# Rotary swap of the first K and Q0 moved from TensorE products to VectorE half-by-half multiplies, with the splits, V rows and first projections reordered

## The reference

```python
Q = (x @ Wq.T + bq); K = (x @ Wk.T + bk); V = (x @ Wv.T + bv)   # per head: 32, 8 and 8 heads of 16
def rot_half(x):
    x1, x2 = jnp.split(x, 2, axis=-1)
    return jnp.concatenate([-x2, x1], axis=-1)
Q, K = q * cos + rot_half(q) * sin, k * cos + rot_half(k) * sin
w = softmax(Q @ K.T / 4)                       # four query heads per key/value head
x = layernorm(x + (w @ V) @ Wo.T + bo)
g = (x @ gate_w.T) * gate_s; u = (x @ up_w.T) * up_s
x = layernorm(x + ((silu(g) * u) @ down_w.T) * down_s)
```

## Time and profile before

| | |
|---|---|
| three runs | 1046.08, 1048.31, 1048.65 us |
| the profiled execution | 1047.48 us, its span 1045.6 us |
| PE busy | 1021.3 us (98%), 5858 matmul records |
| DVE busy | 795.0 us (76%) |
| ACT busy | 666.4 us (64%) |
| POOL busy | 278.5 us (27%) |
| mean granted TensorE clock | 0.995 |
| the chain that ended last | PE 92%, DVE 3%, DMA 2%, ACT 2% |

### The profile page before, as it was taken

The page is one execution under the profiler, slowest core; times in us unless marked ns, Lnnn a source line. Parts: engine busy times, 40 slices in busy tenths (PEclk is TensorE's granted clock), DMA queues, the critical chain, the costliest instruction groups (busy, mean ns, idle before and its releaser), DMA issues.

```text
span 1045.6 us, 15699 instructions
## 1 busy us (share of the span) xinstructions
PE 1021.3 (98%) x5858; PEld 536.3 (51%) x5858; DVE 795.0 (76%) x1139; ACT 666.4 (64%) x1346; POOL 278.5 (27%) x287
## 2 busy tenths in 40 slices
PE   8999999999999999999999998999999999999996
PEld 3643344433444433443444433333447888888885
DVE  4899978899778899779898898999703575563535
ACT  2359877789778889779666687888762431222221
POOL 2742021151345531246210155454000000000002
PEclk9999999999999999999999999999999999999999
DMA  5273517233125522444140447521327511312011
GB/s 203 81 209 109 118 36 215 54 98 90 53 65 127 99 81 40 86 100 104 35 79 12 117 149 155 142 81 34 113 81 198 137 41 41 81 45 37 1 40 43
DMA packets 64433, 94.88 MB, mean 91 GB/s; under 512 B 37536, under 2 KB 37920, under 8 KB 62272
## 3 DMA queue, kind: packets, MB, share of 16 engines
q1 hardware_dynamic: 63776, 93.10, 33.9%
q10 hardware_dynamic: 576, 0.72, 0.2%
HBM read 53.95 MB, written 27.00 MB: 77 GB/s over the span
## 4 chain that ended last, share of the span: by engine, by line
PE 92%; DVE 3%; DMA 2%; ACT 2%; issue 0%; SPq 0%; POOL 0%; POOLq 0%; DVEq 0%
PE PS L457 29%; PE PV L476 24%; PE PSA L546 15%; PE PSA L435 6%; PE PS L563 5%; PE PS L374 4%; PE PS L502 2%; PE PSA L502 2%; PE PV L563 2%; PE PSA L374 1%; PE PS L416 1%; ACT Bn L769 1%; DVE nmx L976 1%; DMA wr<-A 1%; DMA mscr<-mrow 1%; DVE nmx L972 1%
## 5 line engine op out<-in xcount | busy, mean ns | idle before, releaser
L769 ACT ACTIVATE Bn<-PS 128x512 f32<-128x512 f32 x1146 | 545.7, 558 | 102.7 <-PE PS L457 91.0
L457 PE MATMUL PS<-Qt,Kt 50*128 50x512 f32 x1146 | 392.0, 436 | 9.5 <-DMA Qt<-mscr 3.0
L435 PE MATMUL PSA<-Kt,Qt 48*128 48x512 f32 x1024 | 386.5, 460 | 1.2 <-DVE Kt L949 0.8
L972 DVE TENSOR_REDUCE nmx<-PSA 128x1 f32<-128x512 f32 x512 | 327.1, 678 | 33.7 <-PE PSA L435 33.7
L457 PEld LDWEIGHTS PS<-Qt,Kt 50*128 50x128 f32 x1146 | 187.3, 184 | 318.4 <-ACT Bn L769 296.8
L976 DVE TENSOR_REDUCE nmx<-PSA 128x1 f32<-128x1024 f32 x256 | 312.2, 1219 | 25.1 <-PE PSA L435 21.4
L476 PE MATMUL PV<-Bn 128*32 128x512 f32 x2048 | 274.2, 607 | 0.0
L435 PEld LDWEIGHTS PSA<-Kt,Qt 48*128 48x128 f32 x1024 | 175.4, 184 | 11.9 <-DVE nmx L972 3.3
L546 PE MATMUL PSA<-x1Th,wr 128*128 128x512 f32 x344 | 135.0, 393 | 1.1 <-DMA wr<-A 0.5
L546 PE MATMUL PSA<-x1Tl,wr 128*128 128x512 f32 x344 | 134.7, 392 | 0.0
L805 ACT ACTIVATE sg<-PSA,gs 128x512 f32<-128x512 f32 x43 | 29.6, 690 | 128.6 <-PE PSA L546 128.5
(11 more groups left out here) (167 smaller groups left out, 890.4 us busy)
## 6 DMA issues: line engine op xcount, KB each, us to landing
Qt<-pscr SPq DMA_DIRECT2D x90, 128.0 KB, 5.2
A<-in_wf SPq DMA_DIRECT2D x11, 768.0 KB, 7.1
wr<-A SPq DMA_DIRECT2D x33, 256.0 KB, 2.8
pscr<-A SPq DMA_DIRECT2D x16, 512.0 KB, 3.5
vscr<-Bn SPq DMA_DIRECT2D x32, 256.0 KB, 3.0
Kt<-pscr SPq DMA_DIRECT2D x90, 64.0 KB, 2.8
A<-A SPq DMA_DIRECT2D x16, 256.0 KB, 3.7
Bn<-vscr SPq DMA_DIRECT2D x8, 512.0 KB
```

What stands on the lines that cost most here:

```text
L435: op = e.matmul(PSA[:, 2 * s + h, :], Qt[n % 3][p:p + NC_, g % 2, 128 * qt:128 * qt + 128], Kt[n % 3][p:p + NC_, 512 * h:512 * h + 512], s ...
L457: e.matmul(PS2[:, i, cols], Kt[n % 3][rows, 128 * kt:128 * kt + 128], Qt[n % 3][rows, g % 2, 512 * qh + cols.start:512 * qh + cols.stop], ...
L769: e.activation(Pb[c % NP_][:, cols], PS2[:, score_bank[c, p], cols], ACT.Exp, scale=0.25).then_inc(*act_exp.next(piece(c, p)))
L972: e.tensor_reduce(col, slot_pair(s)[:, h, :], AX.X, ALU.max, negate=True).then_inc(*dve_max[s].next((k, 0) if h == 0 else k))
```

## The change

It takes the four permutation products away, with the matrix `swap` and its load. VectorE now exchanges the halves itself: `turn_pairs` multiplies partitions 0 to 63 of `raw` and of `sinT` and writes to partitions 64 to 127, and the other way round; the sign then is the other, so the add becomes a subtract. For (1,1) ACT makes two copies of 64 partitions from `raw`.

It moves `low_first(1, 0)` on DVE ahead of the placing of K. On ACT `round_x` of x comes piece by piece from the start of the program, `round_w(1)` stands ahead of the rounding of (1,0), and `evacuate(0, 1)` behind it. On POOL `low_x` starts with the first x, the wait for `dve_lo` is gone, and `low_w(1)` and `low_x(4, 5)` follow the third `cosines`. On PE a second product of ones with 256 columns stands behind the first one, two V rows stand ahead of the first group of maxima, the other six behind the first two groups, and the 16 projection steps are dealt out by twos and ones from the third group on. The picks of (1,1) use banks 1 and 3, and the first half of V bank 1.

```diff
-            def swap_pairs(i, h, ps):
-                w.wait_ge(*act_ev.at(("first", i, h)))
-                w.wait_ge(*landed["swap"].at())
-                e.matmul(ps, swap, cols_of(i, h)[0], start=True, stop=True).then_inc(*pe_swap.next((i, h)))
...
             e.matmul(PV[:, :], Vflat[:, 0:128], Vflat[:, 0:512], start=True, stop=True)
+            e.matmul(PV[:, 0:256], Vflat[:, 0:128], Vflat[:, 0:256], start=True, stop=True)
...
+            first_jobs = itertools.product(range(2), range(2), range(KT))
+            for k in range(8 + LEAD):
                 advance(4)
+                for t in range(3 * k + 2, 3 * k + 5) if k < 2 else ():
+                    value_rows(0, t, (1, 0)[t // 4])
                 if k == 4:
-                    for a, i in ((0, 2), (1, 3)):
+                    for a, i in ((0, 1), (1, 3)):
+                        clear(bank_free[i])
                         pick(1, 1, 2 + 2 * a, bank(i), pool_cs.at("lo"))
                         bank_free[i] = act_pick.at(("q", 1, a))
...
+                for _ in range((0, 0, 2, 2, 1, 2, 1, 2, 2, 1, 2, 1)[k]):
+                    j, h, part = next(first_jobs)
+                    project_half(j, h, ((2, 3), (0, 3))[j][h], (part,))
...
+            def swap_last():
+                raw, qrot, _, _ = cols_of(1, 1)
+                w.wait_ge(*act_ev.at(("first", 1, 1)))
+                for p in (0, 64):
+                    e.copy(qrot[64 - p:128 - p, :], raw[p:p + 64, :]).then_inc(*act_ev.next("swapped"))
...
-                w.wait_ge(*pe_swap.at((i, h)))
+                w.wait_ge(*act_ev.at(("first", i, h)))
                 w.wait_ge(*landed[f"sin{h}"].at())
-                e.tensor_tensor(qrot, ps, sin, ALU.mult).then_inc(*dve_rope.next(("swap", i, h)))
+                for p in (0, 64):
+                    e.tensor_tensor(qrot[64 - p:128 - p, :], raw[p:p + 64, :], sin[p:p + 64, :], ALU.mult).then_inc(
+                        *dve_rope.next(("swap", i, h)))
                 w.wait_ge(*dve_rope.at(("swap", i, h)))
                 w.wait_ge(*pool_cs.at((i, h)))
-                e.tensor_tensor(raw, rc, qrot, ALU.add).then_inc(*dve_rope.next((i, h)))
+                e.tensor_tensor(raw, rc, qrot, ALU.subtract).then_inc(*dve_rope.next((i, h)))
...
             e.memset(Vflat, 1.0).then_inc(*pool_one.next())
+            low_x(0, 1)
             cosines(0, 0, rcos[0])
+            low_x(2)
             cosines(1, 0, rcos[2])
+            low_x(3)
             cosines(0, 1, rcos[1])
-            w.wait_ge(*dve_lo.at((0, 1)))
             low_w(1)
-            low_x(0, 1)
+            low_x(4, 5)
```

More of the change, by code:

```diff
@@ L115, in post_ln_layer @@
         bo = A[:, 13312:13824]
-        swap = A[:, 13824:13952]
         sel_in = A[:, 13952:14720]
@@ L622, in tensor @@
             e.matmul(PV[:, :], Vflat[:, 0:128], Vflat[:, 0:512], start=True, stop=True)
+            e.matmul(PV[:, 0:256], Vflat[:, 0:128], Vflat[:, 0:256], start=True, stop=True)
             fill(0, 0, 0, 1, 2, 3)
[L624 to L629 removed]
+            fill(1, 0, 0, 1, 2, 3)
+            fill(0, 1, 0, 1, 2, 3)
             pick(0, 0, 0, PSA[:, 0, :], dve_lo.at((0, 0)))
[L631 to L632 removed]
+            fill(1, 1, 0, 1)
             for a in range(2):
                 pick(1, 0, 2 + 2 * a, bank(2 * a), dve_lo.at((1, 0)))
[L635 removed]
+            fill(1, 1, 2)
             pick(0, 1, 0, PSA[:, 1, :], dve_lo.at((0, 1)))
[L637 removed]
+            fill(1, 1, 3)
+            bank_free[0], bank_free[2] = act_pick.at(("q", 0, 0)), dve_pick.at(("q", 0, 1))
             first_rows = [[act_pick.at(("k", 1)), dve_pick.at(("k", 1)), act_pick.at(("q", 0, 0)), dve_pick.at(("q", 0, 1))],
                           [act_pick.at(("q", 1, 0)), act_pick.at(("q", 1, 1))]]
+            for t in range(2):
+                value_rows(0, t, 1)
             w.wait_ge(*act_pick.at(("k", 1)))
@@ L876, in scalar @@
             load(bqk[:, :], bqk_d, "bqk")
-            load(swap, sw_d, "swap")
             load(sel_in.rearrange("p (m c) -> p m c", m=6), sel_d, "sel")
+            round_x(0, 1)
             evacuate(0, 0)
@@ L881, in scalar @@
             e.copy(sel[:, :, :], sel_in.rearrange("p (m c) -> p m c", m=6)).then_inc(*act_pick.next("sel"))
+            round_x(2)
             round_first(0, 0, dve_rope.at((0, 0)))
             evacuate(1, 0)
+            round_x(3)
+            round_w(1)
+            round_first(1, 0, dve_rope.at((1, 0)))
             evacuate(0, 1)
             place(Kt[0][0:NC_, 0:512], PSA[0:NC_, 0, :], pe_pick.at((0, 0, 0)), ("k", 0))
-            round_first(1, 0, dve_rope.at((1, 0)))
+            round_x(4, 5)
             round_first(0, 1, dve_rope.at((0, 1)))
             place(Qt[0][:, 0, 0:512], bank(0), pe_pick.at((1, 0, 2)), ("q", 0, 0))
+            place(Kt[0][0:NC_, 512:1024], PSA[0:NC_, 1, :], pe_pick.at((0, 1, 0)), ("k", 1))
             evacuate(1, 1)
-            place(Kt[0][0:NC_, 512:1024], PSA[0:NC_, 1, :], pe_pick.at((0, 1, 0)), ("k", 1))
-            round_w(1)
-            round_x(0, 1)
-            w.wait_ge(*pe_swap.at((1, 1)))
-            e.copy(cols_of(1, 1)[1], PV[:, :]).then_inc(*act_ev.next("swapped"))
+            swap_last()
+            round_x(6, 7)
+            round_w(2)
             round_first(1, 1, pool_cs.at("rope"))
-            round_x(2, 3, 4, 5, 6, 7)
-            round_w(2)
             round_w(3)
-            for a, i in ((0, 2), (1, 3)):
+            for a, i in ((0, 1), (1, 3)):
                 place(Qt[0][:, a, 512:1024], bank(i), pe_pick.at((1, 1, 2 + 2 * a)), ("q", 1, a))
@@ L1235, in vector @@
                 maximum(next(steps))
-                if k in (2, 4):
-                    add_values(0, k // 4, k // 4)
+                if k in (1, 3):
+                    add_values(0, k // 2, (1, 0)[k // 2])
             for u in range(SPLIT):
@@ L1439, in gpsimd @@
                 *pool_cs.next("lo"))
-            low_x(2, 3, 4, 5, 6, 7)
+            low_x(6, 7)
             low_w(2)
@@ L1812 @@
         "ident": np.eye(128, dtype=np.float32),
-        "swap": np.roll(np.eye(128, dtype=np.float32), 64, 0),
         "sel": select_rows(),
```

47 lines of the change are left out of this document (8 added, 39 removed).

## The result

The changed kernel takes 1054.63 us (median of four runs, 1052.23 to 1054.98), the kernel before on the same chip 1047.91: ratio 1.0068, 95% interval [1.0055, 1.0081]. The profiled execution took 1054.41 us, its span 1052.6 us, 7.0 us more than the span before.

A forecast was written before the change was run, and what follows sets the result against it. PE is full from the main loop on, so its start decides. +4.2 (first maxima) +2.4 (clock) -2.0 (sweep) +1.0 (ACT's wait) = +5.6 on 1047.5, 1053.1, put at 1053.5 for the median; range 1043.3 to 1056.8 us.

The forecast's parts named there:

- Rival 1: DVE's meetings with POOL in the opening cost little: turns of 3.6 us, 1043 to 1044.7 us, faster; chance 0.25.
- Rival 2: DVE gets both multiplies in before POOL: turn 4.8 us, first maxima near 29, 1047.5 to 1051 us; chance 0.17.
- rival 3: Larger loss: POOL's instructions shut DVE out, or half clock lasts into sweep: +8 to +10, 1056 to 1058 us; chance 0.08.
- The multiplies: DVE in the opening: two of 0.69 us each per turn; without POOL a turn takes 3.6 us against 4.7.
- POOL between the turns: DVE's turns in the opening: DVE and POOL wait for each other, so turns take 5.8 us, the third 7.2.
- The series of turns on ACT: Opening: ACT evacuates (1,0) and (0,1) only behind the rounding of the piece before; called new, given no separate size.
- The second product of ones: PE at the program's start: filled idle time brings the clock's rise forward, 1.0 us; first fill ends at 10.6.
- First maxima: End of the opening's first part: 32.3 us against 28.1, so +4.2, with the clock's fall counted separately.
- the clock: PE's idle times in the opening bring half clock on picks, fills and V rows: +2.4 us, bounds 0 and 3.
- The sweep: From first maxima to main loop: 32.7 us against 34.7, so -2.0.
- What is late next: Start of the main loop: ACT waits 1.1 us for Q1's rotation with the exponentials queued behind, +1.0.

The follow-up runs named there:

- e1: The change with POOL's later splits (low_x(2) on, low_w(1)) put back behind the wait for DVE's remainder of (0,1); 1049.76 us, ratio 1.0021.
- e3: The change with POOL's later splits back behind the wait for DVE and evacuate(0, 1) on ACT ahead of the rounding of (1,0) again; 1047.65 us, ratio 1.0002.
- e7: The kernel before with only the three exchanges of (0,0), (1,0), (0,1) made by DVE multiplies instead of permutation products; 1047.93 us, ratio 1.001.
- e8: The kernel before with only the second product of ones (256 columns) added behind the first; 1044.5 us, ratio 0.9986.
- e4: The change with unread products of ones in PE's two long waits, ahead of the picks of (1,0) and (0,1); 1052.01 us, ratio 1.0046.
- e2: The change with evacuate(0, 1) on ACT again ahead of the rounding of (1,0), and round_w(1) behind it; 1054.78 us, ratio 1.0075.
- e6: e3 with the sweep dealt as in the kernel before; 1046.08 us, ratio 0.9996.
- e9: The kernel before with the second product of ones, low_x(0, 1) early on POOL, early rounding on ACT and a new dealing of the sweep; 1043.24 us, ratio 0.9964.
- e11: e3 with two unread products of 128 columns behind each group of maxima from the sixth on; 1046.56 us, ratio 1.0002.

## Why the prediction was right, point by point

The forecast was 1053.5 us, slower by 0.5%, through DVE and POOL standing in each other's way; measured were 1054.63. The direction and the mechanism hold. The kernels e1 and e3 show it by taking POOL's splits away: with all multiplies kept, DVE's last remainder ends at 24.35 and 24.58 us instead of 29.09, and the first maxima come at 27.71 and 27.95 instead of 33.85. What remains untested is the other half of the guard's worth: the kernel before with its permutation products and an unguarded POOL was not run. Rival 1 (the meetings cost little) is out by the rows of 1.65 and 3.42 us. Rival 2, both multiplies first, did not occur either: DVE's pair took 2.36 us even in the first turn. Of rival 3 its second half did come in small, half clock in the sweep, though in the projections and not in the V rows. That the total came out within 1.2 us is partly luck, since several terms below miss by about 1 us and more, in opposite directions. By its own steps:

- **The multiplies.** 0.69 us for 64 partitions was right: a pair that POOL leaves alone takes 1.40 (e7). The gain of 1.1 us per turn was not: with the cosines alone against it a turn is 4.5 us (e1, from DVE's start at 10.64 to 15.11), against 4.7 before.
- **POOL between the turns.** Forecast 5.8, 5.8 and 7.2 us from the evacuation's end to the remainder's; measured 5.45 (11.30 to 16.75), 5.7 (16.61 to 22.29) and 6.9 (22.16 to 29.09). I had every instruction wait for the next end of the other engine; a few were clear, such as the subtract of the second turn. The price per meeting had been read from two rows of which the second, at 1036.14, is a TENSOR_SCALAR and no TENSOR_TENSOR; the rows of the change now show it for the instruction in question: the subtract of the first turn, begun at 13.73, ends at 15.38, 0.55 us behind the end of POOL's at 14.83, as the remainder of the earlier trace rows did behind 22.43. The rule in the Trainium skill ("SBUF — State Buffer", section "Who interferes with whom"), that two SBUF inputs on VectorE and a GpSimd instruction that reads SBUF shut each other out whole, whichever is first, agrees: 1.65 in place of 0.69 us is a wait of 0.96 inside POOL's 1.27, and POOL's 1.72 is its 1.28 and a wait of 0.44.
- **The series of turns on ACT.** In the opening it cost nothing by itself. With it (e1) the first maxima came at 27.71, without it (e3) at 27.95. The times, 1.0021 and 1.0002, leave open whether it costs something elsewhere.
- **The second product of ones.** Forecast 1.0 us, first evacuation at 10.6; it started at 10.61. By itself it was worth 1.9 to 2.0 us in e8's opening. As the sum needed, so it came, and that is luck: the same edit gave a start anywhere from 9.82 to 10.77 us.
- **First maxima.** Forecast 32.3 us and 2.4 for the clock, measured 33.85. Three terms were mis-sized and cancelled in part. The turns ended 0.8 us sooner (29.09, not 29.9). Two V rows are 16 records, 1.95 us at full clock (e1), and I had put 1.0, the price of one. The clock cost 1.4 us on this path, not 2.4 (e4): the picks of (1,0) ran at half clock too, but nobody waited for them.
- **The sweep.** This is the term with the largest miss. Forecast -2.0, measured -0.5 (33.85 to 68.04 is 34.19, against 34.70). About 1.1 of the difference is the half clock at 55.71: its group step took 2.67 us (55.71 to 58.38) where the like one behind it took 1.59 (59.49 to 61.08). The walk group by group was nearly right: in e1 and e3, which have the same dealing and a granted clock of 1.00 from 36 to 60 us, the sweep took 32.95 and 32.94 us, where 32.7 were forecast. What the term lacked is the half clock.
- **What is late next.** Forecast +1.0 for ACT behind Q1's rotation. In the change the rotation ended at 73.13 and ACT took it at 73.78 without waiting for it; ACT had been kept by PE, which waited 0.41 us for DVE's maxima. The rotation came 39.3 us behind the first group, as forecast (39.0); the sweep in front of it had not become shorter. From the loop's start to the rounding it took 5.74 us instead of 5.19, so +0.55 by another wait. The forecast one came in e2 and e3, 0.54 and 0.51 us.
- **Behind the main loop's start** I had put nothing, and 1.2 us came there. A row for each of two moments, the change first:

```profile
644.75 0.20 DVE L997 STREAM_TRANSPOSE mrow<-msp 128x32 f32<-128x32 f32 x1
...
656.02 0.46 PE L451 MATMUL PS<-Qt,Kt 50*128 50x512 f32 x1 [3.50 <-DMA Qt<-mscr]
...
670.94 0.20 DVE L997 STREAM_TRANSPOSE mrow<-msp 128x32 f32<-128x32 f32 x1
```

```profile
638.23 0.20 DVE L1006 STREAM_TRANSPOSE mrow<-msp 128x32 f32<-128x32 f32 x1
...
663.67 0.20 DVE L1006 STREAM_TRANSPOSE mrow<-msp 128x32 f32<-128x32 f32 x1
```

The change is 6.52 us late at the first moment and 7.27 at the second. So 0.7 of the 1.2 us had come before the first, and these were not followed. Between the two moments the wait for the maxima of batch two took 3.50 us instead of 2.98; the other 0.2 us were not followed either. In e1 that stretch went the other way, with a wait of 2.63 us and a granted clock of 0.93 from 640 to 665 us where before and change have 0.86. From one transpose to the other the profiled executions took 23.58 (e8) to 26.87 us (e4), against 25.44 in the kernel before. Why was not tried. Against the kernel before it moves a version by between 1.9 us less (e8) and 1.4 us more (e4), and it is one reason why the main loop's start and the time don't agree better than that.

The sum of the parts that I had named was +5.6 us, and +7.0 were measured on the profiled execution: turns and first maxima +5.7 (forecast 6.6 with the clock), sweep -0.5 (-2.0), rounding of Q1 +0.55 (+1.0), later +1.2 (0).

Two things stay open. What brings the half clock in the last part of the sweep and at the start of the main loop was not found: in the profiled executions the change and e4 have it in the sweep, e1, e2, e3 and e6 at the start of the main loop, e7, e8 and e9 in neither place. The dealing is not it (e6), and filling PE takes it away (e11). And why e1's runs spread over 7.5 us and e3's over 5.6 is not explained.

## What to carry to other kernels

Before a product is moved from PE to DVE, look at what POOL does in the same stretch: an instruction with two SBUF inputs beside a busy POOL took up to 2.4 times as long here (1.65 instead of 0.69 us), and a guard that holds POOL's background work back (here one wait and the order behind it, worth 4.9 us by the ratios of the change and e1) belongs to the change. Be careful with taking away work that PE does while it waits: in e7 it became an idle time of 2.79 us with half clock behind it, and cost 1.0 us at the first maxima. Try the small parts of a change one by one: here one line gained 1.5 to 1.9 us while the whole change lost 7.
